# Spreading the routing weights of a mixture-of-experts stage by DMA instead of by a matmul

## The reference

```python
logits = input @ Wg                                   # 8 experts
top_vals, top_idx = top_k(softmax(logits), 2)
scores = top_vals / sum(top_vals), at the two chosen experts, 0 elsewhere
h = relu(input @ W1[e] + b1[e])                       # 256 hidden columns
y = h @ W2[e] + b2[e]
x = x + tanh(g_ffn[0]) * sum over e of scores[e] * y
```

## Time and profile before

| | us |
|---|---|
| median of three runs | 745.79 |
| lowest and highest of them | 743.23 and 746.12 |
| the profiled execution | 744.32 |
| its span, first to last instruction | 742.5 |
| PE busy in the span | 641.1 |
| DVE busy | 557.7 |
| ACT busy | 426.2 |

### The profile page before, as it was taken

One profiled execution on the slowest core, in us unless ns is written; L12 is line 12 of the kernel. 1 busy time (PEld: TensorE's weight loads), 2 busy tenths in 40 slices (PEclk: granted clock), 3 DMA queues, 4 the chain that ended last, 5 costly groups with the idle time before them and its releaser, 6 DMA issues.

```text
span 742.5 us, 12635 instructions
## 1 busy us (share of the span) xinstructions
PE 641.1 (86%) x4078; PEld 499.9 (67%) x4078; DVE 557.7 (75%) x1275; ACT 426.2 (57%) x665; POOL 103.9 (14%) x131
## 2 busy tenths in 40 slices
PE   5676574899999999998599999989997399999996
PEld 3565453687787787776377766767665277888884
DVE  3766656698898898888478787677776678888885
ACT  4233221477777777776277767667665145555553
POOL 3444321020000000000400122022022100000000
PEclk9667765799999999999699999999999689999998
DMA  5313100000000000001244233412400000000000
GB/s 164 104 55 108 33 9 0 1 0 1 1 0 0 0 0 0 0 29 44 69 107 124 73 78 98 124 42 81 114 1 1 1 0 1 15 15 27 14 15 28
DMA packets 23704, 29.33 MB, mean 39 GB/s; under 512 B 3313, under 2 KB 17522, under 8 KB 23666
## 3 DMA queue, kind: packets, MB, share of 16 engines
q1 hardware_dynamic: 23666, 28.84, 13.8%
HBM read 19.99 MB, written 8.85 MB: 39 GB/s over the span
## 4 chain that ended last, share of the span: by engine, by line
PE 67%; DVE 19%; issue 5%; ACT 5%; POOL 2%; DMA 1%; DVEq 1%; SPq 0%; ACTq 0%; POOLq 0%
PE psum L397 12%; PE psum L398 12%; PE psum L399 12%; PE psum L1247 6%; PE psum L1262 3%; PE psum L1237 2%; DVE c_mx L1418 2%; PE psum L386 2%; DVE xn L326 2%; PE psum L914 2%; DVE c_sm L1424 2%; PE psum L1238 2%; PE psum L1568 2%; DVE stats L294 2%; DVE xl L358 1%
## 5 line engine op out<-in xcount | busy, mean ns | idle before, releaser
L397 PE MATMUL psum<-xh,w_hi 128*128 (+1 forms) x248 | 103.2, 416 | 2.5 <-DVE d_hr L1656 2.1
L1359 ACT ACTIVATE c_pt<-psum 77x512 f32<-77x512 f32 x128 | 74.9, 586 | 52.7 <-PE psum L1247 52.7
L398 PE MATMUL psum<-xl,w_hi 128*128 (+1 forms) x248 | 99.9, 403 | 0.0
L399 PE MATMUL psum<-xh,w_lo 128*128 (+1 forms) x248 | 99.5, 401 | 0.0
L980 ACT ACTIVATE b_hr<-psum,b1s 128x512 f32<-128x512 f32 x128 | 80.8, 685 | 15.6 <-PE psum L399 15.5
L864 DVE TENSOR_TENSOR b_hl<-b_hs,b_hh 128x1024 fp32r<-128x1024 f32 x64 | 78.1, 1221 | 15.4 <-ACT b_hh L858 15.4
L1040 DVE TENSOR_TENSOR b_hs<-b_hr,psum 128x1024 f32<-128x1024 f32 x64 | 77.7, 1214 | 15.5 <-ACT b_hr L980 14.0
L858 ACT ACTIVATE b_hh<-b_hs 128x1024 fp32r<-128x1024 f32 x64 | 67.9, 1061 | 33.2 <-PE psum L399 33.1
L1247 PE MATMUL psum<-ident,c_pf 128*77 128x128 f32 x512 | 73.5, 282 | 0.1
L1418 DVE TENSOR_REDUCE c_mx<-psum 128x8 f32<-128x616 f32 x64 | 50.9, 795 | 22.7 <-PE psum L1238 22.6
L1247 PEld LDWEIGHTS psum<-ident,c_pf 128*77 128x77 f32 x512 | 57.8, 150 | 13.6 <-issue 10.6
(11 more groups left out here) (209 smaller groups left out, 1247.4 us busy)
## 6 DMA issues: line engine op xcount, KB each, us to landing
w_hi<-c_q_spread SPq DMA_DIRECT2D x24, 256.0 KB
stage<-in_weights SPq DMA_DIRECT2D x8, 576.0 KB, 4.2
c_q_spread<-w_hi SPq DMA_DIRECT2D x7, 512.0 KB, 3.3
ctxg<-in_ctxT SPq DMA_DIRECT2D x16, 156.0 KB, 4.3
c_k_spread<-w_lo SPq DMA_DIRECT2D x8, 312.0 KB, 2.2
x_all<-in_x SPq DMA_DIRECT2D x8, 256.0 KB, 2.8
out_dram<-x_all SPq DMA_DIRECT2D x8, 256.0 KB, 2.3
c_kb<-c_k_spread SPq DMA_DIRECT2D x48, 39.0 KB
```

The source lines that it names most:

```text
L397: pe.matmul(o, wh, h, start=start, stop=False)
L398: pe.matmul(o, wh, l, start=False, stop=False)
L399: return pe.matmul(o, wl, h, start=False, stop=stop)
L1359: a_.activation(pt[:, q % NC4, :], bank[2 + q % 2][0:S2, :], ACT.Copy).then_inc(pt_done, 1)
```

## The change

For groups 1 to 7 of stage b the spread matmul is gone. DVE places a third copy of the weights in `ss`, the sum of high and low parts (after.py L844). After the same turn on PE, ACT first copies these 8 rows out of PSUM into `lt_s` (L856), then `st` as before. SP stores the 8 rows to DRAM in two halves and loads each row back, spread over 128 partitions, into one of two places `b_bc` (`SLOTS = 2`): one load for each expert. The load of expert e waits for scale(e-2), which frees its place; the second half of the store waits likewise, for scale(6) of the group before. Scale reads `b_bc` in place of PSUM. The `st` copy stays, for the bias matmuls. Group 0 is as before.

For room, the results have one buffer for two, `bo_all` and `ones_row` reuse setup weights that are no longer read, and the buffer above stage b's grows. The context load of group 0 of stage c is issued at the head of SP's new part.

```diff
-        bo_all = sb("bo_all", [P, P])
-        ones_row = sb("ones_row", [1, P])
+        bo_all = w_wq0
+        ones_row = w_wk0[0:1, :]
...
-                 y=sb("b_y", [P, 2, GT]))
+                 y=sb("b_y", [P, 1, GT]), bc=sb("b_bc", [P, SLOTS, GT]))
...
-                v.tensor_copy(ss[:, p, :, 32:32 + E], sc_l[:, a.tiles(), :].bitcast(F32)).then_inc(self.ss_ready, 1)
+                v.tensor_copy(ss[:, p, :, 32:32 + E], sc_l[:, a.tiles(), :].bitcast(F32))
+                v.tensor_tensor(ss[:, p, :, 64:64 + E], sc_h[:, a.tiles(), :].bitcast(F32),
+                                sc_l[:, a.tiles(), :].bitcast(F32), ALU.add).then_inc(self.ss_ready, 1)
...
                 a_.wait_ge(self.st_ready, a.at(1, 1))
+                if self is xb and not self.first(a):
+                    a_.activation(lt_s[64:64 + E, a.parity, :], misc[64:64 + E], ACT.Copy).then_inc(self.rows_done, 1)
                 a_.activation(st[:, a.parity, :], misc, ACT.Copy).then_inc(self.st_done, 1)
...
+            def step(a, m, t):
+                if not a or xb.first(a):
+                    return
+                p = a.parity
+                sp.wait_ge(xb.rows_done, a.at(1, 0))
+                sp.dma_start(xb.rows_dram[p, 0:4, :], lt_s[64:68, p, :]).then_inc(xb.rows_out[p], 16)
+                xb.before(sp, xb.scaled, a, 0, SLOTS)
+                sp.dma_start(xb.rows_dram[p, 4:E, :], lt_s[68:64 + E, p, :]).then_inc(xb.rows_out[p], 16)
+                for e in range(E):
+                    if e == 0:
+                        sp.wait_ge(xb.rows_out[p], a.pair(32, 32 * p))
+                    else:
+                        xb.before(sp, xb.scaled, a, e, SLOTS)
+                    sp.dma_start(Bb["bc"][:, e % SLOTS, :],
+                                 xb.rows_dram[p, e:e + 1, :].broadcast_to([P, GT])).then_inc(xb.spread_in[e % SLOTS], 16)
...
-                xb.before(pe, xb.scaled, g, e, 2)
-                pe.matmul(SBC[q], sel0[:, e, :], st[:, g.parity, :], start=True, stop=True).then_inc(xb.bc_ready, 1)
+                if xb.first(g):
+                    xb.before(pe, xb.scaled, g, e, 2)
+                    pe.matmul(SBC[q], sel0[:, e, :], st[:, g.parity, :], start=True, stop=True).then_inc(xb.bc_ready, 1)
...
-                xb.before(v, xb.bc_ready, g, e, 0)
+                if xb.first(g):
+                    xb.before(v, xb.bc_ready, g, e, 0)
+                    spread = SBC[q]
+                else:
+                    v.wait_ge(xb.spread_in[e % SLOTS], g.at(64, 16 * (e // SLOTS + 1) - 64))
+                    spread = Bb["bc"][:, e % SLOTS, :]
```

More of the change, by code:

```diff
@@ L445, in dve_setup_late @@
             v.memset(mask_f[:, S2:SK], 0.0)
-            link(v.memset(ones_row[:], 1.0))
+            link(v.memset(ones_row, 1.0))
             v.wait_ge(s_small, 16 * len(small))
@@ L462, in pe_setup_late @@
             pe.matmul(bank[5][:, 0:P], bv1[:].broadcast_to([P, P]), wo1[:], start=True, stop=False)
-            pe.matmul(bank[5][:, 0:P], ones_row[:], bo1[:], start=False, stop=True).then_inc(s_m0, 1)
+            pe.matmul(bank[5][:, 0:P], ones_row, bo1[:], start=False, stop=True).then_inc(s_m0, 1)
         def act_split(a_, a):
@@ L797, in flamingo_kernel @@
         new_scope()
+        SLOTS = 2
         B = dict(hr=sb("b_hr", [P, 2, HC, GT]), hs=sb("b_hs", [P, 2, HC, GT]),
                  hh=sb("b_hh", [P, 2, HC, GT], F32R), hl=sb("b_hl", [P, 2, HC, GT], F32R),
-                 y=sb("b_y", [P, 2, GT]))
+                 y=sb("b_y", [P, 1, GT]), bc=sb("b_bc", [P, SLOTS, GT]))
         class ExpertPass:
@@ L867, in act_y @@
                 a_.wait_ge(self.used, t.at(self.n, self.n))
-                a_.activation(self.y[:, t.parity, :], ybank, ACT.Copy).then_inc(self.y_done, 1)
+                a_.activation(self.y[:, t.parity % self.y.shape[1], :], ybank, ACT.Copy).then_inc(self.y_done, 1)
             def pe_y(self, pe, t, misc):
@@ L872, in pe_y @@
                 for b in range(TG):
-                    ins = pe.transpose(misc[:, b * P:(b + 1) * P], self.y[:, t.parity, b * P:(b + 1) * P], ident[:])
+                    ins = pe.transpose(misc[:, b * P:(b + 1) * P], self.y[:, t.parity % self.y.shape[1], b * P:(b + 1) * P], ident[:])
                 ins.then_inc(self.yt_ready, 1)
@@ L883, in flamingo_kernel @@
         xb = ExpertPass("b", E, B["y"])
+        xb.rows_done, xb.rows_out = sem("b_rows_copied"), [sem("b_rows_stored0"), sem("b_rows_stored1")]
+        xb.spread_in = [sem(f"b_spread_loaded{i}") for i in range(SLOTS)]
+        xb.rows_dram = nc.dram_tensor("b_rows", [2, E, GT], F32).ap()
         Bb = B
@@ L892, in flamingo_kernel, with sp_b @@
         c_prepare = {}
+        def sp_b(sp):
+            c_prepare["sp"](sp)
+            def step(a, m, t):
[13 more added lines that the diff above has]
+                                 xb.rows_dram[p, e:e + 1, :].broadcast_to([P, GT])).then_inc(xb.spread_in[e % SLOTS], 16)
+            pipeline(sp, step)
+        sp_parts.append(sp_b)
         def pe_b(pe):
@@ L1037, in scale @@
                 xb.before(v, xb.z_read, g, e, 0)
-                xb.before(v, xb.bc_ready, g, e, 0)
+                if xb.first(g):
[4 more added lines that the diff above has]
+                    spread = Bb["bc"][:, e % SLOTS, :]
                 xb.before(v, xb.lo_done, g, e, 2)
                 v.tensor_tensor(Bb["hs"][:, q, :, :], Bb["hr"][:, q, :, :],
-                                SBC[q].unsqueeze(1).broadcast_to([P, HC, GT]), ALU.mult).then_inc(xb.scaled, 1)
+                                spread.unsqueeze(1).broadcast_to([P, HC, GT]), ALU.mult).then_inc(xb.scaled, 1)
             def low(g, k):
@@ L1110, in flamingo_kernel @@
         v4 = sb("c_v4", [S2, 2, TG, NH, 2 * VC])
-        above = sb("c_above_b_buffers", [P, 1152])
+        above = sb("c_above_b_buffers", [P, 1664])
         kb0 = sb("c_kb0", [P, NC4, HQ, TG, SK], F32R)
@@ L1157, in route_buffers_c, with sp_c @@
             return route_buffers(sm1[:].rearrange("p a h k -> p (a h k)"), ctxg[:].rearrange("p a k -> p (a k)"))
-        def sp_c(sp):
+        def sp_c(sp, early_only=False):
             def load_context(a):
@@ L1164, in load_context @@
                 sp.dma_start(ctxg[:, a.parity, :], ctxT[:, a.cols(GK)]).then_inc(c_ctx[a.parity], 16)
+            if early_only:
+                load_context(Group(None, 0))
+                return
             def spread_keys(a):
@@ L1196, in step @@
             def step(a, m, t, u):
+                if a and not (a.i is None and a.c == 0):
+                    load_context(a)
                 if a:
-                    load_context(a)
                     spread_keys(a)
@@ L1533, in flamingo_kernel @@
         c_prepare["pool"] = pool_clear
+        c_prepare["sp"] = lambda sp: sp_c(sp, early_only=True)
         c_prepare["read"] = lambda pe: pe.wait_ge(u_read, 2)
```

## The result

The changed kernel takes 752.97 us (median of six runs, 750.67 to 755.08) against 745.95 us of the kernel before in the same series: 1.0094 times, 95% interval 1.0071 to 1.0117. It is slower by some 7 us. The forecast was 739 us, 5 to 7 us faster. The profiled execution took 755.08 us, the slowest of the six; its span is 753.3.

What follows compares the result with a forecast made beforehand. PE was taken to bound the first expert stage's middle groups by its number of matmuls, with VectorE next. 12.9 - 4.3 - 2.0 - 0.8 - 0.5 = 5.3 us off the profiled 744.32 gave 739.0 us, range 735 to 744.5.

Steps and rivals of the forecast that it cites:

- The rule that I set aside: VectorE instructions with two SBUF inputs contend with GpSimd reading SBUF, first comer holding the ports; forecast: trace speaks against it.
- Scale from SBUF: VectorE's scale reading its second operand from SBUF instead of PSUM: costs nothing, as low part takes 1.22 against 1.21 us.
- Rival 4: GpSimd's steps held off by scale(5) and low(4), norm 1.4 us late 6 times: 8 us, 747 us; chance 0.05.
- Rival 3: Spread transfers become the bound for every expert, from a landing of 4.4 us; some 752 us; chance 0.09.
- The gain of the matmuls: PE, groups 1 to 7: 56 removed spread matmuls of 0.23 us each give 12.9 us.
- the slack of VectorE at down(4) and down(5): VectorE's low parts ahead of PE's downs: 0.2 to 0.3 us left at down(4), about nothing at down(5); nothing counted.
- The copy: ScalarE's added copy of 8 rows, 0.48 us, delays PE's result transposes: 0.71 us lost per group, 6 times, 4.3 us.
- The DMA chain: Store then load at a group's start make scale(0) 0.8 us late; 2.0 us over five inner boundaries, bounds 0 and 4.5.
- Rivals 2: Group boundaries cost more, with a landing sum of 5.8 us: 6.9 in place of 2.0 us, 743.9 us; chance 0.20.
- The two outer boundaries: Into group 1 nothing; into group 7 PE waits longer for the normalised rows' low part (L358): 0.8 us.
- The end of the stage: PE's wait for the norm (L326) lengthens after experts 6 and 7, so 0.5 us of gain is worth nothing.
- SyncE's queue into the next stage: Key and query spreads queue behind group 7's last spread, ready at 352.3 with a margin of 1.5 us: costs nothing.

Runs made afterwards that it cites:

- the run with one GpSimd step: Changed kernel with VectorE adding epsilon and GpSimd doing only the power: 744.4 us, ratio to before 0.9992.
- the run with all three edits: Changed kernel with GpSimd doing only the power, rows stored from st without ScalarE's copy, both halves stored before the wait for scale(6): 739.9 us, ratio 0.9918.
- the kernel of the matmuls alone: Kernel before without its 56 spread matmuls, nothing in their place (no copy, no DMA), GpSimd left out of the norm: 740.3 us, ratio 0.9938.
- the fastest one: Changed kernel with GpSimd doing only the power, both halves stored early, ScalarE's two weight copies moved ahead of expert 2's high part: 737.7 us, ratio 0.9882.

## Why the prediction was wrong, point by point

**The rule that I set aside was right for one order: the step that failed.** The term *Scale from SBUF* was put at nothing; it cost 0.85 + 0.47 us at PE in each middle group and, with the last group, some 8 us of the whole time. The prediction looked only at VectorE's own length there, which indeed stayed at 1.22 us. Its paragraph on the rule gave GpSimd's hold 0.05, by one row: low(4), with two SBUF inputs, had started while GpSimd's power ran and took 1.22 us as always. That row shows GpSimd first and VectorE second. The question was the other order, a GpSimd step that starts under a VectorE instruction, and of that the expert stage of the kernel before had no case, since scale(5) read PSUM. The Trainium skill ("SBUF — State Buffer", Who interferes with whom) speaks of both, and the runs bear it out for the order that matters here: 0.18 and 0.22 us became 1.08 and 1.20. For the other order the row of before still stands against it: a VectorE instruction was not held by the power already running, and in the run with one GpSimd step low(4) again took 1.22 us beside a running power. Rival 4 had the mechanism and the mark to look for, though it foresaw one hold till low(4) ends and not one hold for each small step. Its price, 8 us, was near: 1.1 us of each middle group vanish without GpSimd, and some 8 us of the whole time (1.0094 against 0.9986). Rival 3 named some 752 us, close to the 752.97 measured, but by transfers that bound every expert; no such wait is in the trace, so that number met by chance.

**The gain of the matmuls was a third of the term.** 56 x 0.23 = 12.9 us was right as work and wrong as time. I had found the slack of VectorE at down(4) and down(5) to be 0.2 us and nothing, and then counted nothing for it. Taken out alone the matmuls gave 1.0 of 1.86 us per middle group, 3.8 us of the stretch: 0.23 us each went to ScalarE's copy and to VectorE's low(4), 0.4 to small pieces. On the way into group 1, from the first copy of the placed weights to the first result copy, three removed matmuls gave 0.3 us in the run with all three edits (29.85 to 29.57 us) and not 0.7.

**The copy was mis-sized.** Term 0.71 us per group, measured 0.98 (1.21 of waiting against 0.23). The wait was six times and at the place named. ScalarE's copy of 8 rows took 0.61 us from start to start where I took 0.48 from two copies of 128 partitions:

```profile
229.94 1.06 ACT L863 ACTIVATE b_hh<-b_hs 128x1024 fp32r<-128x1024 f32 x1 [0.79 <-PE psum L399]
231.02 0.59 ACT L856 ACTIVATE lt_s<-psum 8x512 f32<-8x512 f32 x1
231.63 0.60 ACT L857 ACTIVATE st<-psum 128x512 fp32r<-128x512 f32 x1
```

and it began 1.08 us after the high part, where the next copy began 0.97 after it before. Why these follow each other later was not tried. And the move of the copy into ScalarE's gap, which the rows already showed as 0.88 us of idle time, was in reach of the prediction.

**The DMA chain was right.** Store and spread in the changed kernel's queue (the second half at 244.51, the first spread at 245.91; landing in the list of issues):

```profile
244.51 0.26 SPq L912 DMA_DIRECT2D b_rows<-lt_s  x1
...
b_bc<-b_rows SPq DMA_DIRECT2D x56, 256.0 KB, 3.0
```

1.4 us for the store of 8 KB, under my bound of 2.0, and 3.0 for the spread, over my 2.8; their sum with the reactions 4.7 where I took 4.9. VectorE waited 0.5 us at scale(0), forecast 0.8, and PE got 0.2 to 0.3, forecast 0.4. Inside a group no expert waited for a spread, as forecast. So the spread of one row of DRAM over 128 partitions landed 0.2 us later than the slowest row of that size. Rivals 2 and 3 are out.

**The two outer boundaries.** The wait for L358 at group 7 grew from 0.58 to 1.37 us, forecast 0.8 more: the number was right. Its reason is not separated: the wait is 1.37 us too in the kernel of the matmuls alone, without GpSimd, and 1.45 in the kernel before with scale from SBUF, with all its matmuls. The end of the stage was put at 0.5 us less gain and cost 2.1 us. The run with both halves stored early has the same wait of 3.17 us for the norm without the fall of the clock, and its last group takes 24.46 us against 23.88 before and 25.97 in the change. So 0.6 us are the norm's delay, and the other 1.5 us are the clock (last section). SyncE's queue into the next stage was right: the key spread issued at 348.74, the query spread at 356.69, and the placing waited for PE's last down till 364.06. The first scores still wait for values.

**The sum.** Term by term per middle group: -1.86, +0.98 (I had +0.71), +0.85 and +0.47 from GpSimd (I had 0), +0.19 at the boundary's down, +0.4 in small pieces: +1.0. Forecast was -0.75.

## What to carry to other kernels

A removed instruction on the bounding engine gives its time only up to the slack of the next engine in the chain: read that slack at each place of the period before counting the removal in full, and take the remainder off the sum. When a second operand of a VectorE instruction moves from PSUM to SBUF, look for the GpSimd steps that start while it runs: here two of 0.2 us became 1.1 and 1.2 us without moving one instruction. And a row clears a rule only for the order of events that it shows; before adding work ahead of a copy that others wait for, look for a gap on that engine where it can go.

## What the runs showed of the hardware that I had not expected

A GpSimd instruction of one element, or of four per partition, that starts under a VectorE instruction with two SBUF inputs is recorded until 0.06 to 0.09 us after that instruction's end: 1.08 us in place of 0.18, and 1.20 in place of 0.22. With the next such VectorE instruction directly behind, the next small step is held again, so three steps in a row are far worse than one (norm 1.24 us late against not at all). A GpSimd step that is already running when the VectorE instruction starts is not held, nor is that instruction: 1.04 and 1.22 us in the kernel before.

In the last group the granted clock can fall. The changed kernel's PE waits 3.17 us for the norm (L326) there, where it was 1.67 us before; the windows of the two stretches behind it:

```profile
354.00:357.00 3.00, 0.81 (x5) 0.81 (x5) 2.07 (x6) 0.17 (x1) 0.98 (x1) 0.85 0.45 104
357.00:360.00 3.00, 3.00 (x10) 2.43 (x9) 2.00 (x3) 0.73 (x2) 0.00 (x0) 0.58 0.67 210
```

and two matmuls in it, 0.43 us apart in place of 0.23:

```profile
358.38 0.63 PE L397 MATMUL psum<-b_hh,w_hi 128*128 128x512 f32 x1
358.81 0.63 PE L398 MATMUL psum<-b_hl,w_hi 128*128 128x512 f32 x1
```

The clock was at its lower level, 1.2 GHz, for some matmuls and returned to 2.4. Before, the same stretch kept 1.00 after its 1.67 us wait. It is not the change alone: the kernel before with one GpSimd step waited 1.93 us there, fell to the same 0.43 us, and its last group took 25.3 us against 23.9, which made up what little it lost (1.0016). The length of the wait does not decide it in this range. After 3.17 us the clock fell in the change and without the copy (last groups of 26.0 and 26.1 us) and not with both halves stored early (24.5). After 2.70 us, with scale from SBUF, it did not fall. After 2.41 or 2.42 us it fell in the kernel of the matmuls alone and in the fastest one (25.3 and 25.2), at less cost in the change without GpSimd and with one GpSimd step (24.5 and 24.1), and not in the three others (23.7 each). What decides it stays open. So single profiles of this kernel carry up to some 1.5 us that come and go with the clock, and I read the middle groups, which agree within some 0.3 us inside a run, for anything smaller.
